# Order of the first blocks' products, weight chunks and row 1's norm at the start of a fused expert and scan kernel

## What is computed

```
xn      = layernorm(x)                                  # over the 128 features
scores  = sigmoid(xn @ router_w.T)                      # 16 experts
combine = top 4 experts inside the best 2 of 4 groups, weights normalised, * 2.5
block k = (silu(xn @ gate_w[k]) * (xn @ up_w[k])) @ down_w[k]
y       = sum over 16 experts of combine[:, k] * block k, plus 2 shared blocks
x       = x + 0.5 * y
```

## Time and profile before

| quantity | value |
|---|---|
| median of three runs | 888.65 us (888.05 to 888.93) |
| profiled execution, its own time | 888.56 us |
| span of its profile | 886.8 us |
| outside the span | 1.76 us |
| TensorE matmul busy | 861.8 us (97%) |
| VectorE, ScalarE, GpSimd busy | 704.3, 555.2, 646.9 us |
| mean granted TensorE clock | 0.998 |

### The profile page before, as it was taken

One profiled execution on the slowest core, in us unless ns is written; L12 is line 12 of the kernel. 1 busy time (PEld: TensorE's weight loads), 2 busy tenths in 40 slices (PEclk: granted clock), 3 DMA queues, 4 the chain that ended last, 5 costly groups with the idle time before them and its releaser, 6 DMA issues. The chain is left out here.

```text
span 886.8 us, 12027 instructions
## 1 busy us (share of the span) xinstructions
PE 861.8 (97%) x3573; PEld 620.3 (70%) x3573; DVE 704.3 (79%) x1234; ACT 555.2 (63%) x1042; POOL 646.9 (73%) x481
## 2 busy tenths in 40 slices
PE   7999999999999999999999997999999999999997
PEld 6778778887867785455545543577887887788885
DVE  5879768777975678999999999776986877786664
ACT  5665565565556668788887884265565556555554
POOL 6858776776766667898898997565767667676765
PEclk9999999999999999999999999999999999999999
DMA  8634474354435253434354334344557436446440
GB/s 211 205 95 144 135 195 119 121 142 132 114 111 141 83 147 98 159 142 141 137 179 151 140 141 148 106 134 124 147 150 197 133 125 143 152 112 174 146 122 24
DMA packets 125138, 122.38 MB, mean 138 GB/s; under 512 B 59272, under 2 KB 82960, under 8 KB 125072
## 3 DMA queue, kind: packets, MB, share of 16 engines
q1 hardware_dynamic: 102368, 116.35, 43.2%
q10 hardware_dynamic: 22704, 5.25, 2.7%
HBM read 112.40 MB, written 9.18 MB: 137 GB/s over the span
## 5 line engine op out<-in xcount | busy, mean ns | idle before, releaser
L777 POOL TENSOR_TENSOR act_lo<-act,act_hi 128x512 fp32r<-128x512 f32 x288 | 372.2, 1298 | 195.3 <-ACT act_hi L883 195.1
L876 ACT ACTIVATE bank<-bank 128x512 f32<-128x512 f32 x252 | 146.7, 582 | 228.0 <-PE bank L1206 218.1
L1102 DVE TENSOR_TENSOR sg<-bank,c_ring 128x512 f32<-128x512 f32 x252 | 172.6, 685 | 96.2 <-ACT bank L876 93.6
L1202 PE MATMUL bank<-x_parts,w_hi 128*128 128x512 f32 x572 | 231.7, 405 | 7.8 <-DVE sg L1102 4.0
L1080 DVE SCALAR_TENSOR_TENSOR act<-sg,bank 128x512 f32<-128x512 f32 x288 | 197.9, 687 | 43.9 <-PE bank L1206 23.4
L1206 PE MATMUL bank<-x_parts,w_hi 128*128 128x512 f32 x572 | 226.2, 395 | 0.0
L1203 PE MATMUL bank<-x_parts,w_lo 128*128 128x512 f32 x572 | 226.2, 395 | 0.0
L883 ACT ACTIVATE act_hi<-act 128x512 fp32r<-128x512 f32 x288 | 179.3, 623 | 0.8 <-PE bank L1178 0.8
L1202 PEld LDWEIGHTS bank<-x_parts,w_hi 128*128 128x128 f32 x572 | 107.5, 188 | 42.5 <-issue 8.7
L1206 PEld LDWEIGHTS bank<-x_parts,w_hi 128*128 128x128 f32 x572 | 107.5, 188 | 25.9
L1203 PEld LDWEIGHTS bank<-x_parts,w_lo 128*128 128x128 f32 x572 | 107.6, 188 | 25.0 <-issue 1.4
(11 more groups left out here) (168 smaller groups left out, 980.0 us busy)
## 6 DMA issues: line engine op xcount, KB each, us to landing
c_ring<-c_dram SPq DMA_DIRECT2D x252, 256.0 KB, 3.8
c_ring<-c_dram SPq DMA_DIRECT2D x64, 512.0 KB, 3.7
y_dram<-out_t SPq DMA_DIRECT2D x56, 64.0 KB, 2.8
y_tok<-y_dram SPq DMA_DIRECT2D x14, 256.0 KB, 3.7
xt_dram<-xn ACTq DMA_DIRECT2D x40, 64.0 KB, 3.3
xt<-xt_dram ACTq DMA_DIRECT2D x10, 256.0 KB, 2.9
out<-x_sb SPq DMA_DIRECT2D x7, 256.0 KB, 2.3
x_sb<-in_L_attn_hidden_states SPq DMA_DIRECT2D x3, 512.0 KB, 5.9
```

The costliest lines, as they stand in the source:

```text
L777: self.nc.gpsimd.tensor_tensor(m["act_lo"][:, g % LAG], m["act"][:, g % ACTS], m["act_hi"][:, g % LAG].bitcast(FP32), ALU.subtract).then_i ...
L876: nc.scalar.activation(self.h_bank[:, g % 2], self.h_bank[:, g % 2], ACT.Silu).then_inc(self.sg_ready, 1)
L1102: nc.vector.tensor_tensor(m["sg"][:, g % 2], silu, weight, ALU.mult).then_inc(self.w_done, 1)
L1202: nc.tensor.matmul(dst, m["w_hi"][:, k, n, :], x_hi, start=True, stop=False)
```

## The change

The first weight chunks are cut smaller (2-4 and 4-6 in place of 2-6), and row 1 of x is loaded behind chunk 2 (blocks 4 and 5) in place of chunk 0. A new function `pe_second_blocks` computes gate and up of blocks 2 and 3 with the low weights last, then the gates of blocks 4 and 5, and the spread comes behind all of it, in `pe_first_blocks`. The warm-up ahead of it is 5 in place of 9. GpSimd makes the low parts of 2-4, of 4-6 and of 6-8 before its first block, row 1's root and shift after block 0, and the low pieces of 8-10, 10-12 and 12-14 after blocks 1, 2 and 3. ScalarE rounds 4-6, 6-10, 10-14 and 14-18 after blocks 1, 3, 4 and 6. VectorE's act(0) and act(1) stand after routing steps 5 and 7 (before: 6 and 9), row 1's statistics behind the routing; row 1's normalisation, transposes and scores come one block later, and its routing starts at block 7 in place of 6.

```diff
-WARM_UP = 14, 2, 1, 9
+WARM_UP = 14, 2, 1, 5
...
                 setup.pool_low_part(pool, 1)
-                norm.pool_root(pool, 1, 1)
-                norm.pool_shift(pool, 1, 1)
                 setup.pool_low_part(pool, 2)
+                setup.pool_low_piece(pool, 0)
                 head = mamba.pool_head(pool)
                 for g, _ in enumerate(f1.pool_blocks(pool)):
-                    if g in (1, 2):
-                        setup.pool_low_piece(pool, g - 1)
+                    if g == 0:
+                        norm.pool_root(pool, 1, 1)
+                        norm.pool_shift(pool, 1, 1)
+                    if 1 <= g < 4:
+                        setup.pool_low_piece(pool, g)
...
-                    if g in (0, 3, 6):
-                        setup.act_high_parts(ae, 2 + g // 3)
+                    if g in HIGH_PARTS:
+                        setup.act_high_parts(ae, 2 + HIGH_PARTS.index(g))
...
-    CHUNKS = [(0, NSH), (NSH, 6), (6, 10), (10, 14), (14, NE)]
-    LO_PIECES = 1, 1, 1, 2, 4
+    CHUNKS = [(0, NSH), (NSH, 4), (4, 6), (6, 10), (10, 14), (14, NE)]
+    LO_PIECES = 1, 1, 1, 2, 2, 4
+
+    LO_AT = {6: (3, 1), 8: (3, 2), 10: (4, 1), 12: (4, 2), 14: (5, 4)}
...
             if n == 0:
-                load_x(1, 2, self.x_loaded[1])
                 sp.dma_start(m["bias_sb"][:, :], m["route_bias"].partition_broadcast(P)
                              ).then_inc(self.bias_loaded, 16)
+            if n == 2:
+                load_x(1, 2, self.x_loaded[1])
...
     def pool_low_piece(self, pool, n):
 
-        a, b = self.CHUNKS[3]
-        self.low_part(self.nc.gpsimd, pool, 3, a + n * (b - a) // 2, a + (n + 1) * (b - a) // 2)
+        chunk, half = 3 + n // 2, n % 2
+        a, b = self.CHUNKS[chunk]
+        self.low_part(self.nc.gpsimd, pool, chunk, a + half * (b - a) // 2, a + (half + 1) * (b - a) // 2)
...
     def pe_wait_parts(self, pe, k):
-        for n, (a, _) in enumerate(self.CHUNKS):
-            if k == a:
-                pe.wait_ge(self.lo_done[n], self.LO_PIECES[n])
+        if k in self.LO_AT:
+            n, pieces = self.LO_AT[k]
+            pe.wait_ge(self.lo_done[n], pieces)
...
-SECOND_ROUTE = ({6: 1, 7: 1, 8: 1, 9: 1, 10: 1, 11: 1, 12: 1, 13: 1, 14: 1, 15: 2, 16: 2},
+SECOND_ROUTE = ({7: 1, 8: 1, 9: 1, 10: 1, 11: 1, 12: 1, 13: 1, 14: 2, 15: 2, 16: 2},
...
-FIRST_ACTS = (6, 9)
+FIRST_ACTS = (5, 7)
+
+HIGH_PARTS = (1, 3, 4, 6)
...
-                if self.p == 0 and g == 3:
+                if self.p == 0 and g == 4:
                     norm.act_apply(ae, 1)
-                if self.p == 0 and g == 4:
+                if self.p == 0 and g == 5:
                     self.act_copy_xt(ae, 1)
-                if g == (2 if self.p else 5):
+                if g == (2 if self.p else 6):
                     self.act_scores(ae, 1, 1)
...
         self.nc.vector.tensor_copy(m["xt"][:, 0], self.misc).then_inc(self.xt_copied, 1)
-        setup.wait_row(dve, 1)
-        norm.dve_stats(dve, 1)
-        norm.dve_aggregate(dve, 1)
         dve.wait_ge(setup.bias_loaded, 16)
         dve.wait_ge(setup.idents, 4)
         for n, _ in enumerate(self.dve_route(dve, 0, 1)):
             if n in FIRST_ACTS:
                 self.dve_act(dve, FIRST_ACTS.index(n))
+        setup.wait_row(dve, 1)
+        norm.dve_stats(dve, 1)
+        norm.dve_aggregate(dve, 1)
...
         self.pe_warm_up(pe, 3, self.misc)
+        self.pe_second_blocks(pe)
+        self.pe_spread_first(pe)
+
+    def pe_second_blocks(self, pe):
+
+        nc, m, setup = self.nc, self.m, self.setup
+        x_hi, x_lo = m["x_hi"][:, 0], m["x_lo"][:, 0]
+        parts = [((self.h_bank, self.u_bank)[n][:, k], NSH + k, n) for n in range(2) for k in range(NSH)]
+        pe.wait_ge(setup.hi_done, 2)
+        for dst, k, n in parts:
+            pe.wait_ge(self.act_ready if n else self.sg_ready, k - 1)
+            nc.tensor.matmul(dst, m["w_hi"][:, k, n, :], x_hi, start=True, stop=False)
+            nc.tensor.matmul(dst, m["w_hi"][:, k, n, :], x_lo, start=False, stop=False)
+        pe.wait_ge(setup.lo_done[1], 1)
+        for dst, k, n in parts:
+            nc.tensor.matmul(dst, m["w_lo"][:, k, n, :], x_hi, start=False, stop=True
+                             ).then_inc(self.u_ready if n else self.h_ready, 1)
+        pe.wait_ge(setup.lo_done[2], 1)
+        for g in range(2 * NSH, 3 * NSH):
+            self.pe_wait_gate_bank(pe, g - 2)
+            self.pe_product(pe, self.h_bank[:, g % 2], 0, g).then_inc(self.h_ready, 1)
...
-                if self.p == 0 and g < NSH:
+                if self.p == 0 and g < 2 * NSH:
                     yield
                     continue
...
-                self.pe_wait_gate_bank(pe, g - 2)
-                self.pe_product(pe, self.h_bank[:, g % 2], 0, g).then_inc(self.h_ready, 1)
+                if self.p or g >= 3 * NSH:
+                    self.pe_wait_gate_bank(pe, g - 2)
+                    self.pe_product(pe, self.h_bank[:, g % 2], 0, g).then_inc(self.h_ready, 1)
...
-                if self.p == 0 and g == 3:
-                    self.pe_spread_first(pe)
-                if self.p == 0 and g == 4:
+                if self.p == 0 and g == 5:
                     self.pe_transpose_xn(pe, 1)
-                if g == (2 if self.p else 5):
+                if g == (2 if self.p else 6):
                     self.pe_logits(pe, 1, 1)
```

More of the change, by code:

```diff
@@ L390, in pool_low_piece @@
     def pool_low_piece(self, pool, n):
-        a, b = self.CHUNKS[3]
-        self.low_part(self.nc.gpsimd, pool, 3, a + n * (b - a) // 2, a + (n + 1) * (b - a) // 2)
+        chunk, half = 3 + n // 2, n % 2
+        a, b = self.CHUNKS[chunk]
+        self.low_part(self.nc.gpsimd, pool, chunk, a + half * (b - a) // 2, a + (half + 1) * (b - a) // 2)
     def dve_low_piece(self, dve, n):
-        a = self.CHUNKS[4][0] + n
-        self.low_part(self.nc.vector, dve, 4, a, a + 1)
+        a = self.CHUNKS[5][0] + n
+        self.low_part(self.nc.vector, dve, 5, a, a + 1)
     def pe_wait_parts(self, pe, k):
-        for n, (a, _) in enumerate(self.CHUNKS):
-            if k == a:
-                pe.wait_ge(self.lo_done[n], self.LO_PIECES[n])
+        if k in self.LO_AT:
+            n, pieces = self.LO_AT[k]
+            pe.wait_ge(self.lo_done[n], pieces)
     def act_high_parts(self, ae, n):
```

## The result

In 20 runs of each kernel the changed kernel took a median of 891.15 us (889.59 to 893.88) and the kernel before 887.42 (886.74 to 889.46). The ratio of the two is 1.0037 (95% interval 1.0029 to 1.0045), so the change costs about 3.3 us; the medians by themselves lie 3.7 apart. The profiled execution took 891.91 us, its span 890.2. The forecast was 890.7, 2.1 slower: the right side and the right path, with a difference a third too small.

What follows compares the result with a forecast made beforehand. The start was taken as bounded by weights, then VectorE's load in blocks 7 to 11. GpSimd's wait spends the 1.8 us lead and w(11) comes 2.1 later: 888.56 + 2.1 = 890.7 us, range 888.2 to 892.0.

Steps and rivals of the forecast that it cites:

- The lead to the spread: TensorE's start: spread at 19.25, ending at 22.7, so the up of block 4 comes 1.8 us earlier.
- GpSimd's hold: GpSimd's piece of 6-8 waits for ScalarE's rounding until 20.45; 15.4 us of work then put act(7) near 35.9, against 34.68.
- Rival 2: GpSimd's piece of 6-8 starts early, so the lead of 1.8 passes through VectorE's stretch: 886.5 us, chance 0.12.
- the rule for the turning point: Start of GpSimd's piece of 6-8 decides: at 18.4 nothing changes, at 16.3 2.1 us are won.
- VectorE, blocks 7 to 11: VectorE from act(7) to w(11) takes 11.8 us against 11.0; w(11) at 47.8, 2.1 us later.
- an upper bound with one more piece held: VectorE's stretch in blocks 7 to 11 with one more low piece held by GpSimd: +2.7 us.
- the start of the sum: The kernel before's profiled execution, 888.56 us, to which 2.1 was added; it lay 0.1 below the median of 888.65.
- The check from TensorE's side: TensorE's fillers and gaps at the start: 7.2 us before, 9.35 after, counting warm-up, downs and gates of blocks 10 to 13.
- Rival 1: VectorE's low pieces in blocks 7 to 11 are not held by contention with GpSimd: +0.9, 889.5 us, chance 0.22.
- Rival 4: TensorE's clock falls to 1.2 GHz at the new gaps, +2.3 to +3.5 on top: 893 to 894 us, chance 0.03.
- the upper half: VectorE's low pieces are held as often as GpSimd works, favouring the higher part of +0.9 to +2.7 us.
- both bounds of VectorE's term: VectorE, blocks 7 to 11: +0.9 us if neither doubtful instruction is held, +2.7 if one more piece is held.

Runs made afterwards that it cites:

- The early rounding: Changed kernel with ScalarE rounding weights 6-10 behind block 1 in place of block 3: 886.75 us, ratio 1.0001 to the kernel before.
- the three later profiles: Changed kernel unaltered, profiled again, once timed beside the others (median 891.21 us, ratio 1.0041) and twice as a single execution: 889.42, 891.01 and 890.32 us.
- the short form: Changed kernel unaltered, executions whose first VectorE low piece takes about 1.2 us and last 0.55: 889.42, 891.01 and 890.32 us.
- the long form: Changed kernel unaltered, execution whose first VectorE low piece takes 2.4 us and last 1.66: 891.91 us.
- the fillers: Changed kernel with 11 filler matmuls on TensorE in the gap ahead of the gate of block 10: 890.25 us, ratio 1.0038 to the kernel before.
- moving the pieces one block later: Changed kernel with VectorE's four low pieces in blocks 8 to 11 in place of 7 to 10: 889.11 us, ratio 1.0018 to the kernel before.
- the late pieces in the kernel before: Kernel before with VectorE's four low pieces of weights 14-18 moved to blocks 11 to 14: 886.61 us, ratio 0.9990.

## Why the prediction was right, and where it was short

- *The lead to the spread* was as worked out: act(1) at 15.23 (15.3), the spread at 19.40 (19.25), the up of block 4 at 22.89 (22.7), so a lead of 1.7 us.
- *GpSimd's hold* was as worked out: piece of 6-8 at 20.52 (20.45), act(7) at 36.04 (35.95). The early rounding shows that it is the cause: with the piece at 16.62 the loss is gone. Rival 2 had put the start at which 2.1 us are won at 16.3. In row 0's turn counted from MAX8 that run won 1.2 us over the kernel before, but its median is only level with it. It did not win the 2.1 us that the rule for the turning point gave such a start, so the rule was right in direction and too generous.
- *VectorE, blocks 7 to 11*, had 11.8 us in the sum. The first of the three later profiles shows 47.74 - 35.93 = 11.8 and block 13 at 48.47, where 48.5 was forecast. In the first profile it was 49.49 - 36.04 = 13.45. This is the term that was mis-sized: I kept the held piece at the 1.22 us of the earlier trace rows, and an upper bound with one more piece held for some 0.6. In that profile the first piece was held for two GpSimd instructions (2.40 us, 1.2 above the short form). The last piece took 1.66, where in the short form it is the norm's shift ahead of it that is held (0.84 us in the first of the three later profiles, then 0.55 for the piece); from shift to w(11) it is 1.65 us against 1.23. The two differences, 1.2 and 0.4, are the whole of 13.45 - 11.8, and the 0.4 is probably the clock's, as above.
- *The further 1.2 us of the median* (3.3 in place of 2.1) stay open, with two candidates. The first is the long form: it costs 1.65 us, so it would have to come in some 0.7 of the executions. For it speak the runs of up to 893.9 us and the 2.0 us (1.7 by the ratios) of moving the pieces one block later, of which the short form accounts for 1.0 (55.2 us from MAX8 to the turn against 54.2). Against it, four of five profiles of the changed order (three later ones, the fillers) had the short form, and the three without fillers took 889.42, 890.32 and 891.01, on average 3.0 above the kernel before without any long hold. The second is the start of the sum: 888.56 was a slow execution of the kernel before, 1.1 above its median of twenty, and one in which chunk 1 came late. A typical gap there may be shorter than the 3.11 us that the change removes. One profile of the kernel before can't tell.
- *The check from TensorE's side* came to 9.35 by luck in its parts. In the first later profile the downs cost 3.1 us in starts, where 3.9 were counted, and the gates of blocks 10 to 13 3.2, where about 2.5 were.
- *Rival 1* (no contention, +0.9): the order with no held piece, one block later, has block 13 at 47.85 with a start 0.4 later, and the turn 1.15 us behind that of before, counted from MAX8. That is near the bound, but not a clean test of it: one piece less stands ahead of w(11) there (0.55 us), and the shift is still held.
- *Rival 4* (the clock): it did fall, at a gap I had said would not come, since I had no gap above 2 us in my list. Directly it cost at most 0.3 us, through act_lo(9) probably 0.4, and nothing like the 2.3 to 3.5 of the rival.
- *The Trainium skill's* sentence on interfaces shared by GpSimd and VectorE (GPSIMD Engine Reference, 1. Specifications) was taken as a reason for the upper half. The traces agree wherever a low piece started while GpSimd was at work on 512 columns: the piece did not slow down by a share, it ended about 0.4 us behind the end of a GpSimd instruction. Where the piece started first, it was GpSimd's instruction that took longer. So "as often as GpSimd works" was too strong: with the late pieces in the kernel before, the first piece was not held, and the act_lo that started 0.04 us behind it took 1.66 in place of 1.29:

```profile
43.35 0.54 DVE L384 TENSOR_TENSOR w_lo<-stage,w_hi 128x384 fp32r<-128x384 f32 x1
```

```profile
43.39 1.66 POOL L779 TENSOR_TENSOR act_lo<-act,act_hi 128x512 fp32r<-128x512 f32 x1 [0.39 <-ACT act_hi L885]
```

My chances put 0.47 on no change within 0.2% and 0.41 on slower; with the rows at hand slower deserved more, since both bounds of VectorE's term lay above zero, though the lower one (+0.9) was still within the 0.2%.

## What to carry to other kernels

A lead won ahead of the first bound is worth what the next one lets through: before moving work forward, list for every engine what now stands in front of its next wait, as GpSimd's piece of 6-8 stood here in front of the whole chain of act_lo. In strict queues put work that waits for a late input behind the short work that others wait for, or make its input earlier; here one number in HIGH_PARTS decides 3 us. And place VectorE's instructions of two SBUF inputs where GpSimd rests.

## What the runs showed of the hardware

- A VectorE subtraction of 384 columns with both inputs in SBUF took 0.52 to 0.55 us where it wasn't held. Where it started during a GpSimd instruction of 512 columns (1.3 us) it mostly took 0.99 to 1.66, and once 2.40 when a second followed without a gap; it ended about 0.4 us behind GpSimd's end. Where it started first (by 0.04 us at 43.35), it took 0.54 and GpSimd's instruction 1.66. The multiplies with one input in a matmul bank (0.68 us) were not held in the same stretches.
- The same instruction stream took either one or two GpSimd instructions of hold in different executions. With one, VectorE's piece ran at their boundary and the second GpSimd instruction took 1.60 us; with two, the second took its 1.29. What decides was not tried.
- A gap of 3.11 us in TensorE left the granted clock at 1.00; ahead of it TensorE had run without a gap from 8.98 to 14.30 us. One of 3.01 us, ahead of which it had already stood still for 0.68 us at 35.3, was followed by 0.81 and 0.77 in the two stretches of 4 us from 40 us on. In that fall the 512-column matmuls were 0.43 us apart in place of 0.23.
